# Rope attention: the next sequence's x turned in four banks, between the last group's values and sums

## The reference

```python
Q = (x @ W_q).reshape(b, s, N_HEADS, HEAD_DIM).transpose(0, 2, 1, 3)
K = (x @ W_k).reshape(b, s, N_KV_HEADS, HEAD_DIM).transpose(0, 2, 1, 3)
V = (x @ W_v).reshape(b, s, N_KV_HEADS, HEAD_DIM).transpose(0, 2, 1, 3)
Qr = _apply_rope(Q, positions)
K_rep = jnp.tile(K, (1, rep, 1, 1))
V_rep = jnp.tile(V, (1, rep, 1, 1))
Kr = _apply_rope(K_rep, positions)
scores = jnp.einsum('bhqd,bhkd->bhqk', Qr, Kr) / HEAD_DIM ** 0.5
weights = jax.nn.softmax(scores, axis=-1)
out = jnp.einsum('bhqk,bhkd->bhqd', weights, V_rep)
out = out.transpose(0, 2, 1, 3).reshape(b, s, d)
return out @ W_o
...
x = _layernorm(x + _L0_attn_ref(x, L0_attn_W_q, L0_attn_W_k, L0_attn_W_v, L0_attn_W_o), axis=-1)
x = _layernorm(x + _L0_xattn_ref(x, ctx_1024, L0_xattn_Wq, L0_xattn_bq, L0_xattn_Wk, L0_xattn_bk), axis=-1)
```

## Time and profile before

| | |
|---|---|
| median of three runs | 2493.07 us |
| the profiled execution's own time | 2491.76 us |
| its span | 2490.0 us |
| mean granted clock of TensorE | 0.951 |
| PE busy | 2164.6 us, 87% |
| DVE busy | 1423.2 us, 57% |
| ACT busy | 1258.6 us, 51% |
| POOL busy | 1017.3 us, 41% |
| first stage | 0 to 530 us: PE busy 455.06, DVE 320.80, ACT 266.62, POOL 202.84 |

### The profile page before, as it was taken

The page is one execution under the profiler, slowest core; times in us unless marked ns, Lnnn a source line. Parts: engine busy times, 40 slices in busy tenths (PEclk is TensorE's granted clock), DMA queues, the critical chain, the costliest instruction groups (busy, mean ns, idle before and its releaser), DMA issues. The chain is left out here.

```text
span 2490.0 us, 33458 instructions
## 1 busy us (share of the span) xinstructions
PE 2164.6 (87%) x12629; PEld 1546.5 (62%) x12664; DVE 1423.2 (57%) x2130; ACT 1258.6 (51%) x2385; POOL 1017.3 (41%) x726
## 2 busy tenths in 40 slices
PE   5989898968896797787999999999999999977782
PEld 4555555536785666565777777777777777744340
DVE  3656666645555435543566765566556665552637
ACT  3636363633425636544555565556655565541413
POOL 2424252511003202203666666666666666530101
PEclk9999999988997999998999999999999999988796
DMA  3000000010001000002111111111111111020001
GB/s 113 1 1 1 1 1 1 1 64 1 1 1 50 1 1 1 1 2 78 51 51 51 60 51 51 47 47 47 48 51 52 51 51 52 18 70 31 1 1 68
DMA packets 60552, 79.14 MB, mean 32 GB/s; under 512 B 6052, under 2 KB 40228, under 8 KB 60392
## 3 DMA queue, kind: packets, MB, share of 16 engines
q1 hardware_dynamic: 60392, 76.99, 9.3%
HBM read 72.78 MB, written 4.19 MB: 31 GB/s over the span
## 5 line engine op out<-in xcount | busy, mean ns | idle before, releaser
L2133 PE MATMUL banks<-s_probsT,s_v 128*128 128x512 f32 x512 | 230.1, 592 | 0.0
L594 DVE TENSOR_REDUCE s_neg_max<-banks 128x1 f32<-128x512 f32 x256 | 165.5, 685 | 89.4 <-PE banks L660 88.0
L2039 DVE RECIPROCAL s_inv_sums<-banks 128x512 f32<-128x512 f32 x64 | 214.2, 3346 | 2.3 <-PE banks L2143 2.3
L1964 ACT ACTIVATE s_probsT<-banks,s_minus_bound,s_qk_rstd 128x512 f32<-128x512 f32 x256 | 186.4, 784 | 11.8 <-PE banks L200 11.8
L543 ACT ACTIVATE s_probsT<-banks 128x512 f32<-128x512 f32 x256 | 148.7, 600 | 81.4 <-PE banks L674 79.1
L1993 DVE TENSOR_REDUCE s_mean_sq<-x_cur 128x8 f32<-128x1024 f32 x64 | 78.1, 1220 | 184.9 <-ACT x_cur L1932 174.4
L1860 POOL TENSOR_TENSOR s_qk_rstd<-s_mean_sq,minus_half 128x8 f32<-128x8 f32 x64 | 105.1, 1642 | 145.8 <-DVE s_mean_sq L1996 142.5
L198 PE MATMUL banks<-s_w_proj_hi,xT_hi 128*128 128x256 f32 x512 | 157.9, 308 | 2.9 <-DVE s_w_proj_lo L2016 2.9
L2133 PEld LDWEIGHTS banks<-s_probsT,s_v 128*128 128x128 f32 x512 | 96.9, 189 | 97.6 <-issue 84.9
L482 POOL TENSOR_TENSOR x_cur<-s_probsT 128x512 f32<-128x512 f32 x64 | 82.0, 1282 | 158.3 <-PE banks L692 109.9
L200 PE MATMUL banks<-s_w_proj_hi,xT_lo 128*128 128x256 f32 x512 | 145.4, 284 | 0.0
(11 more groups left out here) (422 smaller groups left out, 6270.6 us busy)
## 6 DMA issues: line engine op xcount, KB each, us to landing
s_w_proj_raw<-l1x_wq SPq DMA_DIRECT2D x32, 512.0 KB, 3.4
s_w_out_raw<-l1x_wo SPq DMA_DIRECT2D x32, 512.0 KB, 3.6
s_w_proj_raw<-l1x_wk SPq DMA_DIRECT2D x32, 256.0 KB, 2.8
s_w_proj_raw<-l1x_wv SPq DMA_DIRECT2D x32, 256.0 KB, 3.0
x_all<-x SPq DMA_DIRECT2D x4, 1024.0 KB, 12.0
s_ctxT<-ctxT SPq DMA_DIRECT2D x8, 512.0 KB, 4.7
out<-x_all SPq DMA_DIRECT2D x4, 1024.0 KB, 4.3
s_probsT<-l0a_wqkv SPq DMA_DIRECT2D x1, 1536.0 KB, 9.6
```

What stands on the lines that cost most here:

```text
L594: dve.tensor_reduce(nmax[:, h % 2, t, 0:1], ps.ap(s), AX.X, ALU.max, negate=True) \
L1964: act.activation(probs[:, h, k, :], ps.ap(("E", j, h, k)), ACT.Exp, bias=bound[:, 0:1], scale=rs[:, 1, k, h:h + 1]).then_inc(ps.freed(("E" ...
L2039: dve.reciprocal(inv[:, h, :], ps.ap(("SU", j, h))).then_inc(ps.freed(("SU", j, h)), 1)
L2133: mm = pe.matmul(ps.ap(key), v[:, k, h * DX:(h + 1) * DX], probs[:, h, k, :], start=(k == 0), stop=(k == T - 1))
```

## The change

The four blocks of turned x get four banks, 0 to 3, in place of two, 2 and 3. The transposes move out of `project` into a function `turned`. For the first sequence it is called where the transposes stood. For the three others it is called inside `heads` of the sequence before, right after the first value piece of the last group, ("o", 3, 0, 0).

```diff
-            "project": c.x_uses([2, 3]) + [(("p", t), (0, 3)[t % 2], 2) for t in range(T)],
+            "project": c.x_uses([0, 1, 2, 3]) + [(("p", t), (0, 3)[t % 2], 2) for t in range(T)],
...
-            def project(b, pos, heads_before):
+            def turned(b, pos):
                 if b > 0:
                     pe.wait_ge(x_in[b], 16)
                 for k in range(KD):
...
                     mm.then_inc(ps.filled(("x", k)), 1)
+
+            def project(b, pos, heads_before):
+                if b == 0:
+                    turned(0, pos)
                 c.wait_xT(pe, pos)
...
+                    if s == ("o", NKV - 1, 0, 0) and b < B - 1:
+                        turned(b + 1, at("project", b, 1))
```

## The result

| | before | after |
|---|---|---|
| median | 2493.38 us of 4 runs (2491.44 to 2494.36) | 2478.57 us of 4 runs (2477.70 to 2478.69) |
| ratio, 95% interval | | 0.9941 [0.9924, 0.9958] |
| profiled execution, its span | 2491.76, 2490.0 | 2477.70, 2475.9 |
| mean granted clock | 0.951 | 0.950 |

The predicted time was 2478.4. Beside another set of before's runs the changed kernel had the ratio 0.9940 [0.9927, 0.9953]. 14.8 us are gone; between the two profiled executions it is 14.1.

The account below looks back on a forecast made before the run. PE was taken to set the pace, with waits in the turn of x at three sequence boundaries. Boundaries 12.0, clock 1.6 and first turn 0.5 sum to 14.1 us saved, giving 2478.4 us; range 2474 to 2486.

Parts of the forecast that it names:

- The boundaries: Between two sequences, last group's first value to projection: 11.40 us becomes 7.40, 4.00 us gained at each of three, 12.0.
- What is late next: After the boundary's waits go: DVE's quotients, ahead of the first rope, come next but end 1.0 us early.
- POOL's slack of 1.10: At the boundary: POOL's last addition ends at 133.09, 1.1 us before the moved value matmuls end at 134.19.
- DVE's quotients: On DVE between subtractions and first rope: all four end at 140.3, the first projected tile comes at 141.3.
- Rival B: At the boundaries: moved work meets a new wait, POOL's addition or exponentials ending late; costs 4.2 us, 2482.6; chance 0.11.
- The clock: At the first projection: the fall to 1.2 GHz goes with PE's idle before it, 1.59 us gained, between 0 and 4.8.
- The first turn: At the kernel's start: four banks remove PE's 0.56 us wait, so ACT copies the weights earlier; 0.5 us gained.
- Rival C: After the boundaries: 9 or more of the 14 us are waited away in the next sequence; 2490.5, chance 0.07.
- Rival D: Between scores and projection: the clock falls inside the new order of values, transposes and sums; 13.4 us slower, 2505, chance 0.03.

Follow-up runs that it names:

- the experiments with one part each: Against the kernel before: four banks with the turn in its old place, ratio 0.9998; the turn moved but with two banks, 2481.96 us, ratio 0.9955.
- the extra addition: The changed kernel with the first of POOL's two additions for each sequence's last head done twice: 2481.97 us, ratio 0.9961 to before.
- the turn in POOL's gap: The changed kernel with the turn one place later, just ahead of the sums, where PE had waited for POOL: 2477.19 us, ratio 0.9937 to before.
- banks-only kernel: The kernel before with four banks for turned x, the turn in its old place: 2491.90 us, ratio 0.9998; once more 2490.55 us, ratio 0.9996.
- the waits filled: Unread extra transposes in PE's turn waits: in the kernel before, 2490.96 us, ratio 0.9992; in before with four banks, 2488.44 us, ratio 0.9982.
- before with a longer POOL: The kernel before with the first of POOL's two additions for each sequence's last head done twice: 2498.05 us, ratio 1.0032.
- split turn: The changed kernel with the turn's first two blocks moved earlier, ahead of the last head's first transposed score: 2474.27 us, ratio 0.9928 to before; again 2474.38, 0.9926.

## Why the prediction was right, step by step

The time came out as forecast, and its largest term, the boundaries, for the reason given. That it came out to 0.2 us is luck: two changes of 1 us that no term held cancel, as told below.

**The boundaries**, predicted 4.00 us each and 12.0 in all: 4.05, 4.05 and 4.07, 12.17. The durations that were carried over held: 16 transposes from 128.31 to 130.21 are 1.90 us (1.87), first value to projection 7.35 (7.40). The two parts were not split in the prediction; the experiments with one part each split them: the move 2.69, the banks 1.36 more.

**What is late next**: POOL's slack of 1.10 is 1.07 in the trace (131.96 - 130.89) and 0.98 by the extra addition. DVE's quotients end 1.06 us ahead of the tile (1.0). Rival B had its overlap and no price: in the trace POOL's L484 and xT_lo start at 129.61 and 129.63, and take 1.28 us and, all four, 2.48, as they do with the turn in POOL's gap, where they don't overlap and nothing changes. By the Trainium skill (SBUF — State Buffer, "SBUF: two separate sides") a DVE operation takes the shared ports only with two SBUF inputs or in a two-port mode. This pair agrees: xT_lo has one SBUF input and neither is held up.

**The clock**, 1.59 predicted, 1.50 in that stretch of the trace. The size was right, and the idle in the turn as its cause is borne out: the fall at the first projection came in both traces of before and in both of the banks-only kernel, and in none of nine traces with the waits filled or removed (one of them keeps 0.98 us); filled they are in only two, one of each kernel. The idle is not enough for it: before with a longer POOL had the same waits in the turn and no fall at a projection, and the second and third boundary have them in every trace of before without one. Why the first is the one that falls is open. The Trainium skill (TensorE: Matmul & The Clock Gate, Part 1) calls the number of slow matmuls at a kernel's start run-variable. Carried over to falls in mid-kernel, as I did, that does not describe the ones at 141 us; it does describe the one at 177 us, which came in one trace of two.

**The first turn**, 0.5 predicted: 0.81 to ACT's copy. This is the term that was mis-sized. I took the bracket of 0.56 us in the earlier trace rows, but a bracket begins when the last transpose has ended, and its tail is no time in which the next could not be issued. From the first transpose on, the third block was issued 0.76 us late (11.12 - 8.60 before, 9.94 - 8.18 after), and ACT's copy of it began 0.82 late. The first turn gained 1.24 in the two traces, 0.42 of it because x landed earlier in that execution.

**What fell beside the sum**: 0.97 gained in the first sequence's heads and 1.32 lost in the last output product, both at unlike granted clocks, and neither in any term. They nearly cancel, which is luck. They are not alike. The first varies by itself: the banks-only kernel took 107.88 us in one trace and 106.27 in the other. The second came in both traces of the changed kernel (16.97 and 16.95 us, against 15.66 and 15.58 of before), while the kernel with the turn in POOL's gap, whose boundaries are as long, took 15.56. So it goes with the kernel and with where in time that product begins, as far as these five traces tell, and the sum lacked a term of 1.3 us lost there. Rival C, the gain given back later, was false for this kernel but came true in part for the banks alone, where I had not looked for it: given back by the clock, not by DVE.

**Rival D** saw a real mechanism at the wrong kernel: the sums did run slowly, but in the kernel before with one more addition on POOL, behind a wait of 2.24 us. In the changed kernel there is no such wait. Its 2505 is counted from the profiled execution's 2491.76; from the median it would be 2506.5.

## What to carry to other kernels

Work that a later part needs is best placed where its engine waits anyway, with enough independent work behind it to cover the answers of the other engines; write down each slack so won, since it tells how far the next move can go. Banks alone brought nothing clear of noise, while the move needed them to be whole. In this kernel a short wait of TensorE could cost twice, once as itself and once in what ran slowly after it, so count both when a wait is removed, and look for new falls of the clock wherever the change shifts work in time.

## What the runs showed of the hardware

- Most falls of the granted clock to the lower level came back at the same places of the same kernel: at 141 us in both traces of before, at 137 to 140, 298 to 300 and 421 to 423 in both of the banks-only kernel, and over the last output product in both of the changed kernel (16.97 and 16.95 us). Those at 177 us (banks alone) and 288 us (split turn) came in one trace of two. The waits at the three boundaries of a kernel are equal, and yet only the first projection was slow.
- At the first projection a fall followed waits of 0.97 and 1.72 us inside the turn, or one of 2.20; in the kernel with a longer POOL two of three waits of 2.24 us ahead of the sums had one behind them. With extra transposes in the waits there was none, in one trace of each of two kernels.
- What the first stage does not touch varied by itself: from the second stage to the end it took 1955.2 to 1961.4 us over the fourteen traces of this study. A difference of 2 or 3 us in this kernel is read from the edited stretch, not from the whole.
